# Unpacking 4-bit zeros as bytes, fetching the first tiles' scales tile by tile, and forming weights one tile ahead

## The chip, the cores and the metric

The kernel runs on one core of one Trainium2 chip. A core has TensorE (PE, matrix products, results into the eight banks of PSUM), VectorE (DVE), ScalarE (ACT), GpSimd (POOL) and SyncE (SP), which start work when semaphores reach given counts, and 16 DMA engines fed from queues of SyncE, ScalarE and POOL. The metric is the time of one execution on the device, in microseconds; lower is better.

## The reference

Activations x are 4 x 256 tokens of width 512, in f32. The block is a feed-forward, an attention and the same feed-forward again:

```
x = x + 0.5 * ffn(layernorm(x))
x = x + attention(layernorm(x))     # 32 heads of 16, one shared k and v, causal, ALiBi
x = x + 0.5 * ffn(layernorm(x))

ffn(x): w_gu = dequant(qweight_gu, qzeros_gu, scales_gu, g_idx_gu)     # 512 x 2752: gate 1376, up 1376
        w_d  = dequant(qweight_down, qzeros_down, scales_down, g_idx_down)   # 1376 x 512
        return (silu(x @ gate) * (x @ up)) @ w_d
dequant: W[i,j] = scale[g[i],j] * (wq[i,j] - (zq[g[i],j] + 1))
```

The weights wq and the zeros zq are 4-bit numbers, eight to a 32-bit word. Words of qweight hold eight rows of one column; words of qzeros hold eight columns of one group. Gate/up has 4 groups of scales and zeros, down has 10. Both feed-forwards use the same weights.

## The kernel before

**Precision.** Every f32 product is made of three products of reduced f32 ("f32r"): a high half of each operand and the remainder, its low half. `PARTS` (line 1374) lists them as (weight half, activation half): high-high, low-high, high-low. So each weight tile needs a high half (ScalarE's copy) and a low half (VectorE's subtraction), and so do x and the hidden activations.

**Tiles.** The tokens go in two halves of 512, the 1376 hidden columns in 11 tiles of 128 (the last of 96). `s` 0 and 1 are the halves of the first feed-forward, 2 and 3 those of the second. Gate/up weights live in three buffers, `w_near` (tiles 0 to 2), `w_mid` (3 to 6), `w_far` (7 to 10); the last two are also written to memory and read back for the second feed-forward. All weights are dequantised during s = 0, tile by tile, and stay for the rest.

**Preparation.** ScalarE's queue loads the zeros `zw`, the group numbers and, by DRAM to DRAM, the scales into `s_rows` (`scale_rows`, line 616). VectorE unpacks the zeros into 32-bit `zi` one nibble of each word at a time (`unpack`, line 979, eight instructions a call) and casts the near tiles' to bytes `z8` (line 990); ScalarE casts the rest (lines 743, 745). SyncE writes the bytes to `z_rows` and `d_rows`. POOL then gathers, by indirect DMA, one row of scales and one of zeros for each of the 128 partitions and each of 4 k-tiles (`gather_scales`, `gather_zeros`, lines 520 to 528): eight gathers a section, the near one first; `gather_down` (line 530) is one gather a tile, for scales and zeros of the down weight together. A section's tiles can only be formed when all eight of its gathers have landed (`gathered[n]`).

**Forming a tile.** `gu_weight(j)` (line 899) on VectorE shifts and masks the raw words to nibbles (line 906), subtracts zeros and one into PSUM banks 6 and 7 (line 914), multiplies by the scales (line 917). ScalarE's `gu_high(j)` (line 645) casts to the high half; `gu_low(j)` (line 919) takes the low half and frees the banks. `d_weight`, `d_high`, `d_low` do the same for the down weight in SBUF. `load_raw` and `load_raw_d` on SyncE's queue bring the raw words; both, and in iteration 4 the four loads of x's other half (line 398), stand in one order, and each waits for a buffer.

**The order of s = 0**, written out by hand on each engine. VectorE: first the moments and norm of x (`rstds`, `ffn_xn`), x's low halves (`xt_low`), the unpacking of the other zeros, tiles 0 and 1, then in iteration j tile j+2, the product `h_mul(j)` of silu(gate) and up, down weight j, the low halves. TensorE: transposes of x, then for each j `gate_up(0, j)` (24 matmuls of 128x512: for each k-tile the three parts) and `down(0, j-1)` (12). Gate of tile j+1 waits for `sil_ok`, up for `h_ok` of tile j, since one bank each serves gate and up. Its key lines:

```
            for j in range(2):
                gu_weight(j)
                gu_low(j)
            for j in range(NJ):
                if j + 1 < NJ:
                    if j + 2 < NJ:
                        gu_weight(j + 2)
                    h_mul(0, j)
                    d_weight(j)
```

In iterations 3 to 6 VectorE also takes the moments of the next half's x, in 7 to 9 its inverse deviations.

## Time and profile before

| | |
|---|---|
| Runs of the kernel | 614.86, 614.31, 631.7 us; median 614.86 |
| Profiled execution | 614.43 us, of which the span from first to last instruction is 612.6 |
| TensorE matmuls | 559.6 us busy, 91% of the span, 2968 of them |
| TensorE weight loads | 405.8 us, 66% |
| VectorE | 335.8 us, 55% |
| ScalarE | 160.7 us, 26% |
| POOL | 88.9 us, 15% |
| Mean granted TensorE clock | 0.983 of full speed |
| Moved by DMA | 51.52 MB, mean 84 GB/s |

Busy times are of one execution on one core; a line number such as L922 is that of the kernel's text. Matmuls are pipelined, so a busy TensorE need not be at its peak. The releaser of a wait is inferred from semaphore events.

### The profile page before, as it was taken

Reading aid. Unit: us, or ns where it says so; the run is one execution under the profiler, and the core shown is the slowest. Engines: PE = TensorE matmul, PEld = TensorE weight load, DVE = VectorE, ACT = ScalarE, POOL = GpSimd, SP = SyncE. Lnnn points to the kernel's source line nnn. Section 1 sums busy time; section 2 is a strip of 40 time slices with the busy share of each in tenths; the row PEclk is TensorE's granted clock in tenths of the full one; section 3 lists DMA queues with packets and bytes.
Section 4 is the critical chain, followed back from the end, with each engine's and each line's share of the span. In section 5 each row is a group of like instructions: output and inputs, shape, how many; then the busy total and the mean of one; then the engine's idle time right before and its main releaser. Section 6 shows DMA issues by size and latency. Waiting matters only on the chain.

```text
span 612.6 us, 7685 instructions
## 1 busy us (share of the span) xinstructions
PE 559.6 (91%) x2968; PEld 405.8 (66%) x2968; DVE 335.8 (55%) x705; ACT 160.7 (26%) x286; POOL 88.9 (15%) x113
## 2 busy tenths in 40 slices
PE   1399999999999999979799899699999999999997
PEld 1278777778788667656455344356678887888885
DVE  5888999866311355677467899855411245111112
ACT  1242332322111011134523444464111112111110
POOL 4678000000310000021211222131000000000000
PEclk9999999999999999989889999799999999999999
DMA  7489511099057291205843000000790000100001
GB/s 206 152 251 277 147 31 39 13 247 431 8 102 132 76 120 18 39 2 102 144 87 52 4 2 1 6 1 1 237 294 1 1 0 18 51 2 0 1 0 68
DMA packets 40267, 51.52 MB, mean 84 GB/s; under 512 B 10700, under 2 KB 28214, under 8 KB 39832
## 3 DMA queue, kind: packets, MB, share of 16 engines
q1 hardware_dynamic: 35392, 40.13, 26.5%
q0 software_dynamic: 2656, 10.57, 5.4%
q10 hardware_dynamic: 2184, 0.35, 0.4%
q8 instruction: 23, 0.38, 0.3%
q14 instruction: 12, 0.10, 0.0%
HBM read 35.82 MB, written 15.02 MB: 83 GB/s over the span
## 4 chain that ended last, share of the span: by engine, by line
PE 58%; DVE 9%; ACT 1%; DMA 1%; issue 1%; ACTq 0%; DVEq 0%
PE bank L1395 25%; PE bank L1421 12%; PE bank L1561 4%; PE bank L1487 3%; PE bank L1454 3%; DVE nm L1129 3%; PE bank L1479 3%; PE bank L1533 2%; PE bank L1519 2%; PE bank L1554 2%; DMA qp_b<-two 1%; PE bank L1435 1%; PE bank L1439 1%; DVE stats L843 1%; PE bank L1361 1%
## 5 line engine op out<-in xcount | busy, mean ns | idle before, releaser
L1421 PE MATMUL bank<-w_d,hs 128*128 128x512 f32 (+1 forms) x528 | 131.1, 396 | 3.3 <-DVE w_d L944 1.8
L1421 PEld LDWEIGHTS bank<-w_d,hs 128*128 128x128 f32 (+1 forms) x528 | 97.6, 188 | 27.9 <-issue 5.4
L953 DVE TENSOR_TENSOR hf<-sil,bank 128x512 f32<-128x512 f32 (+1 forms) x44 | 30.1, 684 | 151.9 <-PE bank L1395 151.7
L1395 PE MATMUL bank<-xt,w_far 128*128 128x512 f32 (+1 forms) x384 | 92.5, 394 | 0.0
L1395 PE MATMUL bank<-xt,w_mid 128*128 128x512 f32 x384 | 90.6, 391 | 0.0
L1395 PE MATMUL bank<-xt,w_near 128*128 128x512 f32 x288 | 73.3, 406 | 10.0 <-DVE w_near L922 9.4
L1395 PEld LDWEIGHTS bank<-xt,w_mid 128*128 128x128 f32 x384 | 72.0, 188 | 15.4 <-issue 0.5
L1395 PEld LDWEIGHTS bank<-xt,w_far 128*128 128x128 f32 (+1 forms) x384 | 69.3, 181 | 18.2
L1129 DVE TENSOR_REDUCE nm<-bank 128x2 f32<-128x512 f32 (+1 forms) x96 | 61.7, 685 | 31.5 <-PE bank L1487 31.0
L1395 PEld LDWEIGHTS bank<-xt,w_near 128*128 128x128 f32 x288 | 54.2, 193 | 24.5 <-issue 12.2
L674 ACT CAST hs<-hf 128x512 fp32r<-128x512 f32 (+1 forms) x44 | 27.3, 621 | 130.9 <-DVE hf L953 118.0
L664 ACT ACTIVATE sil<-bank 128x512 f32<-128x512 f32 (+1 forms) x44 | 26.3, 597 | 127.8 <-PE bank L1395 127.4
L959 DVE TENSOR_TENSOR hs<-hf,hs 128x512 fp32r<-128x512 f32 (+1 forms) x44 | 32.5, 739 | 19.4 <-ACT hs L674 19.3
L1361 PE MATMUL bank<-ident,xn 128*128 128x128 f32 x96 | 17.2, 327 | 22.3 <-DVE xn L886 21.8
L1188 DVE RECIPROCAL den<-bank 128x128 f32<-128x128 f32 x32 | 30.4, 949 | 9.6 <-PE bank L1554 9.6
L1454 PE MATMUL bank<-xa,wqkv 128*128 128x256 f32 x128 | 31.5, 397 | 0.0
L1361 PEld LDWEIGHTS bank<-ident,xn 128*128 128x128 f32 x96 | 13.1, 166 | 26.4 <-issue 21.1
L608 POOL TENSOR_SCALAR_AFFINE_SELECT pt_a<-pt_a 128x512 f32<-128x512 f32 x16 | 10.4, 648 | 135.9 <-ACT pt_a L727 135.9
L1479 PE MATMUL bank<-causal,ident_b 128*128 128x256 bf16 (+1 forms) x96 | 22.7, 319 | 7.1 <-DVE nm L1129 6.2
L1454 PEld LDWEIGHTS bank<-xa,wqkv 128*128 128x128 f32 x128 | 24.6, 197 | 6.1 <-issue 2.8
L727 ACT ACTIVATE pt_a<-bank 128x512 f32<-128x512 f32 x32 | 17.4, 596 | 37.2 <-PE bank L1519 37.2
L1561 PE MATMUL bank<-wo,at_t 128*128 128x512 f32 x48 | 25.0, 627 | 0.0
(148 smaller groups left out, 566.5 us busy)
## 6 DMA issues: line engine op xcount, KB each, us to landing
gate_up_part<-w_mid SPq DMA_DIRECT2D x1, 4096.0 KB, 15.5
q_rows<-qst SPq DMA_DIRECT2D x16, 256.0 KB, 4.8
w_mid<-gate_up_part SPq DMA_DIRECT2D x4, 1024.0 KB, 8.3
gate_up_part<-w_far SPq DMA_DIRECT2D x1, 3840.0 KB, 24.0
qp_a<-q_rows SPq DMA_DIRECT2D x24, 128.0 KB, 4.4
w_far<-gate_up_part SPq DMA_DIRECT2D x3, 1024.0 KB, 9.0
raw_d<-in_L_ffn_qweight_down SPq DMA_DIRECT2D x10, 256.0 KB, 3.5
x<-in_L_attn_hidden_states SPq DMA_DIRECT2D x8, 256.0 KB, 5.0
```

The lines of the kernel that those rows point to most:

```text
L664: nc.scalar.activation(sil[0:jw(jt(s, p)), n % 2, :], gate_bank(s, p)[0:jw(jt(s, p)), :], ACT.Silu)\
L674: nc.scalar.copy(hs[0:jw(jt(s, p)), n % 2, 0, :], hf[0:jw(jt(s, p)), n % 2, :]).then_inc(h_hi, 1)
L953: nc.vector.tensor_tensor(hf[0:jw(jt(s, p)), n % 2, :], sil[0:jw(jt(s, p)), n % 2, :], up_bank(s, p)[0:jw(jt(s, p)), :], ALU.mult).then_in ...
L959: nc.vector.tensor_tensor(hs[0:jw(jt(s, p)), n % 2, 1, :], hf[0:jw(jt(s, p)), n % 2, :], hs[0:jw(jt(s, p)), n % 2, 0, :].bitcast(F32), ALU ...
L1129: nc.vector.tensor_reduce(nm[:, min(u, 1), 2 * h0 + s:2 * (h0 + heads) + s - 1:2], bank[6 + s][:, :].rearrange("p (h n) -> p h n", h=heads ...
L1188: st.did(nc.vector.reciprocal(den[:, cols], ps))
L1361: ins = nc.tensor.transpose(ps[:, k * P:(k + 1) * P], xn[:, n % 2, k * P:(k + 1) * P], ident[:, :])
L1395: ins = nc.tensor.matmul(ps[0:jw(j), :], w_gu(a, k, gu, j), xt[:, b, k, :], start=(k == 0 and q == 0), stop=(k == KT - 1 and q == 2))
L1421: ins = nc.tensor.matmul(acc(s, t)[:, :], hs[0:jw(j), n % 2, a, t * P:(t + 1) * P], w_d[0:jw(j), j, b, :], start=(p == 0 and q == 0), stop ...
L1454: ins = nc.tensor.matmul(q_bank(b, h)[:, m * S:(m + 1) * S], wqkv[:, k, (2 * h + m) * P:(2 * h + m + 1) * P], xa[:, k, :], start=(k == 0), ...
L1479: nc.tensor.matmul(ps[:, :, 4 * P // heads - P:], ident_b[:, :], causal[:, :].unsqueeze(1).to_broadcast([P, heads, P]), start=True, stop=F ...
L1561: ins = nc.tensor.matmul(out_bank(b, t)[:, :], normed(b)[:, k, t * P:(t + 1) * P], wo[:, k, :], start=(k == 0), stop=(k == KT - 1))
```

## The change

It has four parts. (1) Zeros are unpacked as bytes: two instructions per matrix shift whole words by 0 and by 4 and mask with 0x0f0f0f0f (`unpack`, with a third column of `shifts` that POOL sets to 4), and two strided byte copies interleave them into `z8`. They stand earlier: all gate/up zeros at the very start, down's after the moments of x; ScalarE's byte copies stand ahead of its casts of the transposed x. (2) The scales and zeros of each near tile get a DRAM tensor of their own, `near_rows[j]`, in which a row holds both; POOL fetches tile 0, 1 and 2 with four gathers each (`gather_near`) into `near_raw`, which lies where `w_far` will be, so that the far gathers wait for the near tiles to be formed (`gu_w` at 3). POOL's order is near 0, near 1, down 0, near 2, down 1 and 2, the middle eight, down 3, the far eight, the other down. (3) Weights are formed one tile ahead instead of two: only tile 0 before the loop, tile j+1 in iteration j; the nibbles are split off as `gu_nibbles`. (4) For s = 0 the products of a gate or up go part by part over the four k-tiles in the order high-high, weight high with x low, weight low with x high (`FIRST`), and the waits for low halves move to the part that needs them.

The diff, cut to its core (declarations of buffers and semaphores left out):

```diff
...
+    near_rows = [nc.dram_tensor(f"near_rows{j}", (G_GU, 2, P + P // 4), F32, kind="Internal").ap()
+                 for j in range(SEC[1])]
...
-            sp.wait_ge(z_bytes[0], 1)
+            sp.wait_ge(z_bytes[0], 2)
             z_near = z8[0:2 * G_GU, 0:SECW[0]].bitcast(F32)
-            sp.dma_start(z_rows[0].rearrange("r (g n) -> (r g) n", g=2), z_near).then_inc(z_ok[0], 16)
-            load_raw(0)
+            for j in range(SEC[1]):
+                sp.dma_start(near_rows[j][:, :, P:].rearrange("r g n -> (r g) n"),
+                             z_near[:, j * P // 4:(j + 1) * P // 4]).then_inc(near_ok[j], 16)
+                if j == 0:
+                    load_raw(0)
+            sp.wait_ge(z_bytes[1], 2)
+            for n in (1, 2):
+                cols = z8[0:2 * G_GU, SEC[n] * P:SEC[n] * P + SECW[n]].bitcast(F32)
+                sp.dma_start(z_rows[n].rearrange("r (g n) -> (r g) n", g=2), cols).then_inc(z_ok[n], 16)
+            sp.wait_ge(z_bytes[2], 2)
+            sp.dma_start(d_rows[:, D:D + D // 4], z8[32:32 + G_D, 0:D].bitcast(F32)).then_inc(d_rows_ok, 16)
             load_raw(1)
             load_raw_d(0)
             load_raw(2)
-            sp.wait_ge(z_bytes[1], 1)
-            for n in (1, 2):
-                cols = z8[0:2 * G_GU, SEC[n] * P:SEC[n] * P + SECW[n]].bitcast(F32)
-                sp.dma_start(z_rows[n].rearrange("r (g n) -> (r g) n", g=2), cols).then_inc(z_ok[n], 16)
-            sp.wait_ge(z_bytes[2], 1)
-            sp.dma_start(d_rows[:, D:D + D // 4], z8[32:32 + G_D, 0:D].bitcast(F32)).then_inc(d_rows_ok, 16)
             load_raw_d(1)
...
+            def gather_near(j):
+
+                pool.wait_ge(near_ok[j], 32)
+                for kt in range(KT):
+                    nc.gpsimd.indirect_dma_start(near_raw[:, j, kt, :, :].rearrange("p g n -> p (g n)"), None,
+                                                 near_rows[j].rearrange("r g n -> r (g n)"), group_of(kt))\
+                        .then_inc(near_in[j], 16)
...
-            pool.wait_ge(s_ok[0], 16)
-            for kt in range(KT):
-                gather_scales(0, kt)
-            pool.wait_ge(z_ok[0], 16)
-            for kt in range(KT):
-                gather_zeros(0, kt)
+            gather_near(0)
             pool.wait_ge(gi_d_in, 32)
             groups(slice(KT, KT + NJ), G_D)
             st.wait()
+            pool.wait_ge(d_rows_ok, 32)
+            gather_near(1)
+            gather_down(0)
+            gather_near(2)
+            gather_down(1)
+            gather_down(2)
             pool.wait_ge(s_ok[1], 16)
+            pool.wait_ge(z_ok[1], 16)
             for kt in range(KT):
                 gather_scales(1, kt)
-                if kt == 0:
-                    pool.wait_ge(z_ok[1], 16)
                 gather_zeros(1, kt)
-                if kt == 1:
-                    pool.wait_ge(d_rows_ok, 32)
-                    gather_down(0)
-            gather_down(1)
-            gather_down(2)
+            gather_down(3)
             pool.wait_ge(s_ok[2], 16)
             pool.wait_ge(z_ok[2], 16)
+            pool.wait_ge(gu_w, SEC[1])
             for kt in range(KT):
                 gather_scales(2, kt)
                 gather_zeros(2, kt)
-            gather_down(3)
             for j in range(4, NJ):
...
+            def near_scales(j):
+
+                act.dma_start(near_rows[j][:, :, 0:P], gu3[:, :, j * P:(j + 1) * P]).then_inc(near_ok[j], 16)
...
-            scale_rows(0, slice(0, SECW[0]), slice(0, SECW[0]))
+            near_scales(0)
...
+            for j in range(1, SEC[1]):
+                near_scales(j)
...
+            act.wait_ge(z_unpacked[0], 2)
+            for e in range(2):
+                nc.scalar.copy(z8[0:2 * G_GU, SECW[0] + e:F:2],
+                               zi[0:2 * G_GU, e, :].bitcast(U8)[:, SECW[0] // 2:F // 2]).then_inc(z_bytes[1], 1)
+            act.wait_ge(z_unpacked[1], 2)
+            for e in range(2):
+                nc.scalar.copy(z8[32:32 + G_D, e:D:2], zi[32:32 + G_D, e, 0:D // 8].bitcast(U8))\
+                    .then_inc(z_bytes[2], 1)
             for t in range(4):
                 xt_high(0, t)
-            act.wait_ge(z_unpacked[1], 8)
-            nc.scalar.copy(z8[0:2 * G_GU, SECW[0]:F], zi[0:2 * G_GU, SECW[0]:F]).then_inc(z_bytes[1], 1)
-            act.wait_ge(z_unpacked[2], 8)
-            nc.scalar.copy(z8[32:32 + G_D, 0:D], zi[32:32 + G_D, 0:D]).then_inc(z_bytes[2], 1)
             gu_high(0)
-            gu_high(1)
             for j in range(NJ):
                 silu(0, j)
-                if j + 2 < NJ:
-                    gu_high(j + 2)
+                if j + 1 < NJ:
+                    gu_high(j + 1)
...
+            def gu_nibbles(j):
+
                 dve.wait_ge(raw_in[j % 3], 32 * (j // 3 + 1))
                 words = raw[:, j % 3, 0:2 * jw(j)]
                 st.did(nc.vector.tensor_scalar(words, words, shifts[:, 0:1], low4[:, :].bitcast(I32),
                                                ALU.logical_shift_right, ALU.bitwise_and))
-                dve.wait_ge(gathered[n], 128)
+
+            def gu_weight(j):
+
+
+
+                n, cols = section(j)
+                words = raw[:, j % 3, 0:2 * jw(j)]
+                dve.wait_ge(*((gathered[n], 128) if n else (near_in[j], 64)))
                 if j >= 1:
                     dve.wait_ge(gu_lo, j)
                 st.wait()
                 q = words.bitcast(U8).rearrange("p (g n k) -> p k g n", g=2, k=KT)
                 w = gu_product(j)
-                st.did(nc.vector.scalar_tensor_tensor(out=w, in0=q, scalar=1.0, in1=zs[n][:, :, :, cols],
+                zeros, scales = zs[n], gu_weights(0, j).bitcast(F32)
+                if n == 0:
+                    scales, zeros = near_raw[:, j, :, :, 0:P], near_raw[:, j, :, :, P:].bitcast(U8)
+                st.did(nc.vector.scalar_tensor_tensor(out=w, in0=q, scalar=1.0, in1=zeros if n == 0 else zeros[:, :, :, cols],
                                                       op0=ALU.subtract, op1=ALU.subtract))
                 st.wait()
-                nc.vector.tensor_tensor(w, w, gu_weights(0, j).bitcast(F32), ALU.mult).then_inc(gu_w, 1)
+                nc.vector.tensor_tensor(w, w, scales, ALU.mult).then_inc(gu_w, 1)
...
-            def unpack(n, rows, lo, hi):
-
-                z = zi[rows, 8 * lo:8 * hi].rearrange("p (w e) -> p w e", e=8)
-                for e in range(8):
-                    nc.vector.tensor_scalar(z[:, :, e], zw[rows, lo:hi], 4 * e, 15,
-                                            ALU.logical_shift_right, ALU.bitwise_and)\
-                        .then_inc(z_unpacked[n], 1)
-
+            def unpack(n, rows, words):
+
+                for e, shift in ((0, shifts[rows, 0:1]), (1, shifts[rows, 2:3])):
+                    nc.vector.tensor_scalar(zi[rows, e, words], zw[rows, words], shift,
+                                            low4[rows, :].bitcast(I32),
+                                            ALU.logical_shift_right, ALU.bitwise_and).then_inc(z_unpacked[n], 1)
+
+            dve.wait_ge(four_ok, 1)
+            st.wait()
             dve.wait_ge(z_in, 16)
-            unpack(0, slice(0, 2 * G_GU), 0, SECW[0] // 8)
-            dve.wait_ge(z_unpacked[0], 8)
-            nc.vector.tensor_copy(z8[0:2 * G_GU, 0:SECW[0]], zi[0:2 * G_GU, 0:SECW[0]]).then_inc(z_bytes[0], 1)
+            unpack(0, slice(0, 2 * G_GU), slice(0, WPR))
+            dve.wait_ge(z_unpacked[0], 2)
+            for e in range(2):
+                nc.vector.tensor_copy(z8[0:2 * G_GU, e:SECW[0]:2],
+                                      zi[0:2 * G_GU, e, :].bitcast(U8)[:, 0:SECW[0] // 2]).then_inc(z_bytes[0], 1)
...
+            dve.wait_ge(zd_in, 16)
+            unpack(1, slice(32, 32 + G_D), slice(0, D // 8))
             rstds(0)
             ffn_xn(0, 0)
             ffn_xn(0, 1)
+            gu_nibbles(0)
+            ffn_xn(0, 2)
+            ffn_xn(0, 3)
+            gu_weight(0)
             for t in range(4):
                 xt_low(0, t)
-                if t < 2:
-                    ffn_xn(0, t + 2)
-            unpack(1, slice(0, 2 * G_GU), SECW[0] // 8, F // 8)
-            dve.wait_ge(zd_in, 16)
-            unpack(2, slice(32, 32 + G_D), 0, D // 8)
-            for j in range(2):
-                gu_weight(j)
-                gu_low(j)
+            gu_low(0)
             for j in range(NJ):
                 if j + 1 < NJ:
-                    if j + 2 < NJ:
-                        gu_weight(j + 2)
+                    gu_nibbles(j + 1)
+                    gu_weight(j + 1)
+                    if j == 0:
+                        gu_low(j + 1)
                     h_mul(0, j)
                     d_weight(j)
-                    if j + 2 < NJ:
-                        gu_low(j + 2)
+                    if j > 0:
+                        gu_low(j + 1)
...
+            FIRST = ((0, 0), (0, 1), (1, 0))
...
-                    pe.wait_ge(xt_lo, 4 * (s + 1))
+                    if s:
+                        pe.wait_ge(xt_lo, 4 * (s + 1))
...
-                for k in steps:
-                    if s == 0 and gu == 0 and k == 0:
-                        pe.wait_ge(gu_hi, j + 1)
-                        pe.wait_ge(gu_lo, j + 1)
+                if s == 0:
+                    for q, (a, b) in enumerate(FIRST):
+                        if gu == 0 and q == 0:
+                            pe.wait_ge(gu_hi, j + 1)
+                        if gu == 0 and q == 1:
+                            pe.wait_ge(xt_lo, 4)
+                        if gu == 0 and q == 2:
+                            pe.wait_ge(gu_lo, j + 1)
+                        for k in range(KT):
+                            ins = nc.tensor.matmul(ps[0:jw(j), :], w_gu(a, k, gu, j), xt[:, b, k, :],
+                                                   start=(k == 0 and q == 0), stop=(k == KT - 1 and q == 2))
+                for k in () if s == 0 else steps:
...
```

## Rows read from the trace of the kernel before

**Rows 1.** Waits of 0 to 45 us: who waited for whom, us, times, longest
```profile
PE bank L1395 <- DVE w_near L922: 9.4, 1, 9.4
```
**Rows 2.** Timeline, all engines, 0 to 40 us: start, us, what, idle before
```profile
5.57 1.30 ACTq L618 DMA_DIRECT2D scale_rows<-in_L_ffn_scales_gu  x2
...
8.46 1.22 POOL L523 DMA_INDIRECT w_near<-scale_rows,gidx  x1 [1.13 <-DMA scale_rows<-in_L_ffn_scales_gu]
...
12.05 1.41 DVE L886 TENSOR_SCALAR xn<-x,mv,rstd 128x512 f32<-128x512 f32 x2
...
19.70 2.18 DVE L983 TENSOR_SCALAR zi<-zw 8x124 int32<-8x124 int32 x16
...
22.84 1.24 DVE L914 SCALAR_TENSOR_TENSOR bank<-raw,zs 128x1024 f32<-128x1024 uint8 x1 [0.51 <-DVE raw L906]
...
25.37 1.01 ACT L648 CAST w_near<-bank 128x1024 fp32r<-128x1024 f32 x1 [2.76 <-DVE bank L917]
```
**Rows 3.** Timeline of TensorE's matmuls, 0 to 140 us
```profile
27.79 12.92 PE L1395 MATMUL bank<-xt,w_near 128*128 128x512 f32 x48 [9.36 <-DVE w_near L922]
...
43.79 5.60 PE L1395 MATMUL bank<-xt,w_near 128*128 128x512 f32 x24
49.23 2.88 PE L1421 MATMUL bank<-w_d,hs 128*128 128x512 f32 x12
51.95 5.60 PE L1395 MATMUL bank<-xt,w_mid 128*128 128x512 f32 x24
...
66.87 3.01 PE L1421 MATMUL bank<-w_d,hs 128*128 128x512 f32 x12 [1.17 <-DVE w_d L944]
...
109.74 2.92 PE L1421 MATMUL bank<-w_d,hs 128*128 128x512 f32 x12
...
118.04 1.03 PE L1361 MATMUL bank<-ident,xn 128*128 128x128 f32 x8
```
**Rows 4.** Timeline of VectorE, 40 to 130 us
```profile
41.27 1.23 DVE L914 SCALAR_TENSOR_TENSOR bank<-raw,zs 128x1024 f32<-128x1024 uint8 x1
...
43.67 0.68 DVE L953 TENSOR_TENSOR hf<-sil,bank 128x512 f32<-128x512 f32 x1
...
46.26 1.22 DVE L922 TENSOR_TENSOR w_mid<-bank,w_mid 128x1024 fp32r<-128x1024 f32 x1
...
51.56 0.68 DVE L953 TENSOR_TENSOR hf<-sil,bank 128x512 f32<-128x512 f32 x1
...
58.75 0.42 DVE L906 TENSOR_SCALAR raw<-raw,shifts,low 128x256 int32<-128x256 int32 x1 [2.16 <-DMA raw<-in_L_ffn_qweight_gu]
...
61.71 0.68 DVE L953 TENSOR_TENSOR hf<-sil,bank 128x512 f32<-128x512 f32 x1
...
104.68 0.68 DVE L953 TENSOR_TENSOR hf<-sil,bank 128x512 f32<-128x512 f32 x1
```
**Rows 5.** Timeline, all engines, 0 to 40 us: POOL's gathers and what meets them
```profile
22.00 0.61 SPq L388 DMA_DIRECT2D zero_rows<-z  x2
...
24.41 0.95 POOL L528 DMA_INDIRECT zs<-zero_rows,gidx  x1 [3.29 <-DMA zero_rows<-z]
...
28.12 1.23 DVE L914 SCALAR_TENSOR_TENSOR bank<-raw,zs 128x1024 f32<-128x1024 uint8 x1
28.17 2.00 POOL L534 DMA_INDIRECT w_d<-down_rows,gidx  x1 [0.30 <-issue]
...
34.37 1.06 POOL L528 DMA_INDIRECT zs<-zero_rows,gidx  x1 [0.30 <-issue]
```
**Rows 6.** By tile, 0 to 45 us: landing of the gathers into zs, then w_near
```profile
DMA to landing us min/median/max: 2.6/3.1/6.2
...
DMA to landing us min/median/max: 4.1/4.4/4.9
```
**Rows 7.** DMA issues of 47.4 to 47.5 us: count, KB each, us to landing
```profile
x<-in_L_attn_hidden_states SPq DMA_DIRECT2D x1, 256.0 KB, 5.1
w_far<-scale_rows,gidx POOLq DMA_INDIRECT x1, 8.2
```

29 lines of the change are left out of this document (18 added, 11 removed).

## The prediction

> **What bounds the kernel now.** I read the page first: TensorE has work in 91% of the span (the table above). It is the bound nearly everywhere, so a change outside its stream pays only where it waits. The waits of the first 45 us name one large stop: 9.4 us before the first gate/up matmul, ended by VectorE's low half of tile 0 [rows 1]. The timeline of that stretch shows what stands ahead of it [rows 2]. POOL gathers the scales and zeros of all three near tiles in eight gathers, the first at 8.46. VectorE unpacks the other zeros from 19.70 (16 instructions, 2.18 us), subtracts the zeros at 22.84 and multiplies; ScalarE casts at 25.37, VectorE takes the low half, and TensorE starts at 27.79 [rows 3]. TensorE's own timeline then shows the stage [rows 3]: a tile is 5.44 us of gate/up (43.79 to 49.23) and 2.72 of down (to 51.95), 8.16 together. The gate/up of the last tile is over at 118.04, where transposes start. VectorE's timeline [rows 4] shows why TensorE still waits 1.17 at 66.87: one tile's VectorE work takes 7.89 (43.67 to 51.56), VectorE stops 2.16 for the raw words of tile 5 at 58.75, and where it also does the next half's moments a tile takes 8.59 (61.71 to 104.68, five tiles). So this stage has two bounds, the start and VectorE, and after 118.04 nothing is touched by the change.
>
> **The start.** The unpacking shrinks: 24 instructions of one nibble each become four shift-and-mask instructions on whole words. The first pair (8x172) now covers all gate/up zeros; a 128x256 one of this form took 0.42 [rows 4] and the 8x124 ones 0.14 apiece [rows 2], so 0.25 to 0.4 each; two byte copies follow. That ends near 4, as before, so nothing is won on the first zeros. Gone is the 2.18 at 19.70; instead two small instructions (0.4) come before the norm, and ScalarE's byte copies (at its 1 ns an element, 1.2 and 0.7 a pair) go ahead of the transposed casts: its DMA issues, two more at 0.65, end at 9, its table load at 10.3, the copies at 12.3, and its first cast was at 14. Tile 0 now needs four gathers, not eight. A gather costs POOL 0.95 plus 0.30 whether it carries scales, zeros or both [rows 5], the first a little more: from 8.46 the fourth is issued at 12.5. It lands after 4.1 to 4.9 (the 3072-byte rows) or 2.6 and more (the 768-byte rows) [rows 6]; with 1280-byte rows I take 3.9, so 16.4. VectorE is by then done: its first two normalised tiles end at 13.5 [rows 2], 0.4 later now, one nibble instruction 0.4, two more tiles 0.7 each, that is 15.8 at least and some 16.1 with their waits for transposes. Subtract and multiply 2.5, to 18.9; cast 1.0 and two handoffs, to 20.1. TensorE needs only the high halves first, so it starts at about 20.2, 7.6 earlier. The four xt low halves (2.5) and the weight's low half (1.2) end at 22.7, inside the first eight matmuls, which are the slow ones: the first 48 took 12.92, and two later sets of 24 take 10.9 [rows 3]. Tile 0 ends near 27.6.
>
> **One tile ahead.** Tile 1 must be formed after tile 0's low half. Its gathers wait on POOL for the down rows in memory: ScalarE's copy ends at 12.3, SyncE issues, and such a write took 2.4 from issue at 22.00 to POOL's release at 24.41 [rows 5], so POOL goes on at about 15.2; 20.2 for the fourth, landed at 23, as VectorE arrives. Tile 1 is complete at 28, tile 0's product, down weight and low halves at 32. Then the new order must hold: a low half ends 3.8 after the product of the tile before (43.67 to 47.48 [rows 4]), and TensorE wants it for its third pass 2.72 + 1.81 = 4.5 after the last tile's end. High halves come 1.1 after a weight, before TensorE's 2.72 of down are over. Both hold while VectorE is less than 0.7 behind. Where VectorE is the bound, TensorE ends a tile 3.7 after the low half: a handoff of 0.1, the gate's third pass 0.91, the up 2.72.
>
> **What is late next: the middle section.** Tile 3 needs eight gathers of four tiles' rows. Before, the last was issued at 34.37 as POOL's 17th and landed unseen before 41.27. Now it is the 23rd: from 15.2 there are 19 (eight near, three down, eight middle). At the bare 1.26 the last starts at 37.9. But some take longer: the one that began at 28.17, 0.05 after a VectorE instruction with two operands in SBUF, took 2.00 and ended 0.82 after that instruction; from 24.41 to 34.37 the pitch was 1.42 with one such in seven [rows 5], which for all 19 would give 40.8. Laying the 19 on VectorE's new order, with that 0.82, I find one or two, so 39.3. Landing: up to 6.2 for zeros [rows 6], but 8.2 where the loads of x run beside it [rows 7], and now these loads (SyncE waits for the down weight of tile 1, about 38) do run beside it. I take 5.2, so 44.5; the ends are 41 (37.9 + 3.1, the zeros' middle value) and 49 (40.8 + 8.2). VectorE would have wanted it at 40.5 to 41.
>
> The Trainium skill (SBUF — State Buffer, "SBUF: two separate sides") says that VectorE and GpSimd share a port pair which an instruction holds alone to its end, among VectorE's those with two SBUF inputs against a GpSimd instruction that reads SBUF. The trace agrees with it, by the 2.00 above. Without such holds the last gather would start at 37.9 and the sum come out 1.4 lower.
>
> **The sum.** Tile 3 subtracted at 44.5 instead of 41.27 [rows 4], but by now VectorE is one product further: product 2 at 46.9 instead of 51.56, 4.7 early. The 2.16 at 58.75 goes: the words of tile 5 are asked for in the same place but wanted one tile (8 us) later. Product 3 is then 6.8 early (54.9). From there both kernels run at VectorE's 8.6; product 8 comes at 98.4 (6.3 early: the narrow last tile's weight, 0.5 cheaper, is no longer ahead of it). Low half of tile 9: +3.8; TensorE ends it 3.7 later, 105.9 against 109.74. With the last tile 8.16 it ends at 114.0 against 118.04: **4.0 us off**, since TensorE, whose tiles ended some 4 us ahead of VectorE's product before, is now 1 us ahead. The 7.6 of the start is not what counts. The rest of the span follows unchanged: norms, transposes, loads of attention weights and spills are all triggered from the end of this stage. The profiled execution took 614.43 (span 612.6), 0.4 under the median of the runs shown; 614.43 − 4.0 = 610.4, with the median's share **610.5**.
>
> **Rivals.**
> (a) The middle gathers land by 41 to 42: then VectorE is never stopped, product 2 comes 3 earlier, and the gain is 6.5 to 7.5: 607.5. For it: the bare issue time. Against: the loads of x at that place, and that it leaves nothing for the two-operand instructions.
> (b) They land at 46 to 48.5: each us is a us; gain 0 to 2.5, 613. For it: the 8.2 landing.
> (c) Slower than before. The queue on POOL stretches: if the ten gathers before tile 3 (two down, eight middle) all took 2.00 + 0.30, as single ones did, they would end 10.4 later, land at 55 and cost 10.5: 621. It decides at 48.5; beyond that each us is a us over 614.4. For it: the upper end of 49 is already past that point. Against: the 1.42 of the stretch most like it, one long gather in seven [rows 5].
> (d) Tile 0 doesn't come earlier: four gathers are as late as eight, because the row of scales and zeros of tile 0 isn't in memory until late. The zeros now leave in pieces of 128 bytes, before 384 bytes; the first gather waited 1.13 for the scales, not for them. Losing all 7.6 puts VectorE at tile 2 at 39.6 and leaves 0.4 of the gain: 614. I see nothing that long; up to 4 us lost by VectorE alone at the start cost nothing, since the middle gathers hide them, while what POOL loses there is lost us for us.
> The Trainium skill (DMA: Bandwidth & Descriptors, "Specifications") says that under 512 bytes the engines read, modify and write. Both kernels' zeros are under it, and no row here separates it from the rest of a landing. Its "Rules for kernel authors" would have small transfers joined into large ones; here the trace shows the price as POOL's 1.26 a gather, four more of them, 5 us on the way to tile 3, and that is in the sum.
>
> **How the numbers follow.** Chances: forecast (landing 42.5 to 46) 0.50; (a) 0.20; (b) 0.15; (c) 0.10; (d) 0.05. The range for 8 in 10 takes (a) whole to 7.4 us off and the forecast and (b), and a little of (c): 607.0 to 615.3. Two per cent (12.3 us) is about what a measurement of this kernel can tell from no change: faster by more would need everything of the start (7.6) and all of TensorE's waits after it (under 2) and more, 0.03; slower by more is the far end of (c), landing after 60, 0.02; within, 0.95.
>
> **What would show it.** In the profile after: the first gate/up matmul at about 20 (19 to 22), its wait under 3.5 us; no wait of VectorE for the words of tile 5; a new wait of VectorE before the subtraction of tile 3, ended by the middle gathers, of about 4 us, at 44.5; eight middle gathers issued up to 39 to 40, those begun in VectorE's two-operand instructions longer; TensorE's second gate/up before the down of tile 0 ends at 33; short waits (0.2 to 0.9) before the third pass in the later tiles; the last gate/up of the stage ending at about 114. Wrong would be: tile 3 without a wait (a), tile 2 late because TensorE or ScalarE stands in VectorE's way, or a loss after 118, where I expect a mere shift.

## The result, and the profile after

Recorded were four executions of each kernel, side by side: the changed kernel 630.62, 632.28, 633.57 and 637.12 us (median 632.92), the kernel before 614.31, 614.86, 631.22 and 631.7. The ratio is 1.031 [1.021, 1.040]: **slower**, where 610.5 was forecast, with 0.02 on slower. Two of four executions of the kernel before had lost some 17 us as well; one of them (631.7) was in the table from the start, and the prediction did not ask what it was. The ratio sets the changed kernel against the two executions near 614 alone; beside the two at 631 it is 1.5 us slower in the median. The experiments below ran the kernel before on six more occasions, each on another chip, and the changed kernel on five of them. On three of these chips no execution shows the loss, and there the ratio is 1.003 [1.001, 1.005], 1.002 [1.000, 1.004] and 1.003 [1.001, 1.006]. So there are two results: a **stop** that comes and goes, and that costs the changed kernel some 7 to 20 us an execution, and without it a change that is worth nothing, or 1 to 2.4 us less than nothing, where 4 us of gain were forecast.

TensorE's timeline of the recorded profile (630.62 us, span 628.8) answers to [rows 3]; its columns are start, duration, engine, line, operation, tiles, count and the idle time before:

```profile
19.62 12.89 PE L1439 MATMUL bank<-xt,w_near 128*128 128x512 f32 x48 [2.46 <-issue]
32.35 2.88 PE L1469 MATMUL bank<-w_d,hs 128*128 128x512 f32 x12
36.05 2.06 PE L1439 MATMUL bank<-xt,w_near 128*128 128x512 f32 x8 [0.82 <-issue]
48.10 4.88 PE L1439 MATMUL bank<-xt,w_near 128*128 128x512 f32 x14 [9.99 <-issue]
...
58.36 0.58 PE L1469 MATMUL bank<-w_d,hs 128*128 128x512 f32 x1 [1.72 <-issue]
...
65.38 3.05 PE L1469 MATMUL bank<-w_d,hs 128*128 128x512 f32 x7 [0.81 <-issue]
68.27 5.72 PE L1439 MATMUL bank<-xt,w_mid 128*128 128x512 f32 x24
```

The start is what was forecast: 19.62 (27.79 before), the down of tile 0 at 32.35. Then, from 38 to 66, there are 10 us of nothing, a short run, and single matmuls a microsecond or two apart. (All 24 matmuls of this tile and all 12 of the down are on record, so it is not a gap in the records.) Nothing that the profile shows releases them ("issue"). ScalarE's timeline:

```profile
34.41 0.60 ACT L688 ACTIVATE sil<-bank 128x512 f32<-128x512 f32 x1 [3.79 <-remote]
...
65.55 0.60 ACT L688 ACTIVATE sil<-bank 128x512 f32<-128x512 f32 x1 [17.98 <-remote]
```

and VectorE's:

```profile
44.31 0.69 DVE L987 TENSOR_TENSOR hf<-sil,bank 128x512 f32<-128x512 f32 x1 [9.59 <-remote]
```

ScalarE waits 3.8 and 18.0 us for gate tiles, VectorE 9.6 for tile 1's up, whose last matmul TensorE has on record before 32.4. "Remote" is the profile's word for a signal without a record of who sent it. The windows of the same profile (length; then busy time and count of PE, its weight loads, DVE, ACT and POOL; granted clock, DMA share, GB/s) show who goes on:

```profile
38.00:44.00 6.00, 0.12 (x1) 0.00 (x0) 0.00 (x0) 0.00 (x0) 4.48 (x6) 0.74 0.85 280
44.00:50.00 6.00, 1.90 (x5) 1.51 (x6) 5.42 (x9) 1.24 (x2) 4.48 (x6) 0.50 0.78 240
...
56.00:62.00 6.00, 2.34 (x4) 0.76 (x3) 0.00 (x0) 0.00 (x0) 4.67 (x5) 0.66 0.98 344
```

POOL issues its gathers at the usual pace, the last of them at 60.96, and the DMA engines move 240 to 344 GB/s, while the three compute engines stand or go in short runs. From 68.3 on the profile is that of the changed kernel on a chip without the stop (a_again, below), 14 to 15 us late.

**Where each execution is.** The start of silu is an event that every trace has, 11 a stage. In us, from ScalarE's timelines:

| start of silu of | before | b_again | a_again | a_third | a_fourth | after, recorded | t_tiles | g_late |
|---|---|---|---|---|---|---|---|---|
| tile 0 | 32.98 | 33.10 | 24.51 | 26.36 | 24.53 | 24.36 | 24.22 | 25.07 |
| tile 3 | 54.87 | 55.30 | 56.77 | 52.20 | 55.97 | 71.30 | 48.75 | 56.33 |
| tile 4 | 64.95 | 68.06 | 65.36 | 60.36 | 64.13 | 79.47 | 56.91 | 64.52 |
| tile 8 | 99.46 | 102.56 | 99.49 | 94.60 | 98.28 | 113.64 | 91.23 | 99.18 |
| tile 10 | 115.46 | 118.52 | 116.73 | 111.91 | 115.61 | 130.89 | 108.68 | 116.44 |
| half 1, tile 0 | 129.80 | 132.87 | 131.91 | 128.62 | 130.73 | 146.09 | 125.46 | 131.61 |
| second feed-forward, tile 0 | 420.48 | 424.42 | 422.41 | 420.44 | 421.91 | 436.64 | 417.15 | 422.78 |
| span | 612.6 | 616.5 | 614.5 | 612.5 | 616.1 | 628.8 | 609.2 | 614.9 |

(b_ is the kernel before, a_ the changed one, once more.) The forecast was −4.0 at tile 10 and from there on. a_third has −3.55 there and loses it by the second feed-forward, a_fourth has +0.15, a_again +1.27. Each column is one execution, and two of one kernel can be 3 us apart, as before and b_again are; a_third's is the fastest of its 12. That the change wins nothing rests on all 36 executions of the three chips, not on a column.

### The profile page after: what moved, and what is told of

Its sections match the earlier page's. It is cut to its first block, busy times and chain, and to the rows that moved or that the text cites. A ratio compares the mean times of both kernels' runs of the same rounds, so it can differ in the third digit from the quotient of the medians.

```text
span 628.8 us, 7679 instructions
## 1 busy us (share of the span) xinstructions
PE 564.7 (90%) x2968; PEld 407.6 (65%) x2968; DVE 333.5 (53%) x686; ACT 161.4 (26%) x288; POOL 90.9 (14%) x118
## 4 chain that ended last, share of the span: by engine, by line
PE 57%; DVE 8%; ACT 1%; DMA 1%; issue 1%; ACTq 0%; DVEq 0%
PE bank L1443 25%; PE bank L1469 11%; PE bank L1609 4%; PE bank L1535 3%; PE bank L1502 3%; DVE nm L1167 3%; PE bank L1527 2%; PE bank L1581 2%; PE bank L1567 2%; PE bank L1602 2%; DMA qp_b<-two 1%; PE bank L1483 1%; PE bank L1487 1%; DVE stats L870 1%; PE bank L1399 1%
## 5 line engine op out<-in xcount | busy, mean ns | idle before, releaser
L1469 PE MATMUL bank<-w_d,hs 128*128 128x512 f32 (+1 forms) x528 | 133.8, 400 | 6.9 <-issue 5.5
L1469 PEld LDWEIGHTS bank<-w_d,hs 128*128 128x128 f32 (+1 forms) x528 | 99.3, 190 | 32.6 <-issue 9.7
L1443 PE MATMUL bank<-xt,w_far 128*128 128x512 f32 (+1 forms) x288 | 69.7, 395 | 0.0
L1443 PE MATMUL bank<-xt,w_mid 128*128 128x512 f32 x288 | 68.2, 392 | 0.0
L1443 PEld LDWEIGHTS bank<-xt,w_mid 128*128 128x128 f32 x288 | 54.0, 188 | 11.7 <-issue 0.5
L1443 PEld LDWEIGHTS bank<-xt,w_far 128*128 128x128 f32 (+1 forms) x288 | 51.9, 181 | 13.6
L1443 PE MATMUL bank<-xt,w_near 128*128 128x512 f32 x216 | 54.7, 401 | 0.7 <-issue 0.7
L993 DVE TENSOR_TENSOR hs<-hf,hs 128x512 fp32r<-128x512 f32 (+1 forms) x44 | 32.5, 738 | 19.4 <-ACT hs L698 19.3
L1439 PE MATMUL bank<-xt,w_near 128*128 128x512 f32 x72 | 20.6, 444 | 16.1 <-issue 16.1
```

The lines of the kernel that those rows point to most:

```text
L993: nc.vector.tensor_tensor(hs[0:jw(jt(s, p)), n % 2, 1, :], hf[0:jw(jt(s, p)), n % 2, :], hs[0:jw(jt(s, p)), n % 2, 0, :].bitcast(F32), ALU ...
L1439: ins = nc.tensor.matmul(ps[0:jw(j), :], w_gu(a, k, gu, j), xt[:, b, k, :], start=(k == 0 and q == 0), stop=(k == KT - 1 and q == 2))
L1443: ins = nc.tensor.matmul(ps[0:jw(j), :], w_gu(a, k, gu, j), xt[:, b, k, :], start=(k == 0 and q == 0), stop=(k == KT - 1 and q == 2))
L1469: ins = nc.tensor.matmul(acc(s, t)[:, :], hs[0:jw(j), n % 2, a, t * P:(t + 1) * P], w_d[0:jw(j), j, b, :], start=(p == 0 and q == 0), stop ...
```

## The experiments

"Before" beside each is the kernel before in the same job on the same chip.

### First job (chip 9): both kernels again, and two halves of the change

> The kernel before, unchanged. Two of its four times so far were 614 and two 631; the kernel after showed 631 to 637 and a stop of the engines between 34 and 66 us. Theory A (a stop that some executions of any version have, and that the change does not cause): this control shows both 614 and some 631 again, and its trace at 631 shows idle TensorE of some 17 us within the first 70 us. Theory B (the change itself makes the stop, the two 631 of before are something else, of the chip): at most one in five above 620 here, all of after's above 628.

> The kernel after, unchanged. Theory A: a part of the executions at 609 to 612, the forecast of the schedule without the stop (forecast 114 us for the end of the stage instead of the 133.5 measured), the others at 630 to 637. Theory B: all at 628 or more.

**b_again** 614.8 (12 runs) against 615.17, ratio 0.999 [0.996, 1.001]. **a_again** 617.18 (614.4 to 619.0, 12 runs), ratio 1.003 [1.001, 1.005]. No stop in either: Theory B, that every execution of the changed kernel has it, falls. That the change has no part in it does not follow; see the fourth job. What a_again shows instead is the step that the forecast put in doubt. VectorE's timeline, to be read against [rows 4]:

```profile
39.98 0.42 DVE L930 TENSOR_SCALAR raw<-raw,shifts,low 128x256 int32<-128x256 int32 x1
47.58 1.23 DVE L948 SCALAR_TENSOR_TENSOR bank<-raw,zs 128x1024 f32<-128x1024 uint8 x1 [7.19 <-DMA zs<-zero_rows,gidx]
```

TensorE's, and one window:

```profile
51.28 8.61 PE L1439 MATMUL bank<-xt,w_mid 128*128 128x512 f32 x24 [5.71 <-ACT w_mid L670]
59.73 2.88 PE L1469 MATMUL bank<-w_d,hs 128*128 128x512 f32 x12
62.45 5.60 PE L1439 MATMUL bank<-xt,w_mid 128*128 128x512 f32 x24
```
```profile
50.00:56.00 6.00, 4.72 (x11) 3.83 (x12) 5.70 (x10) 2.15 (x3) 4.78 (x5) 0.55 0.85 274
```

VectorE waits 7.2 us for the middle rows, which land at 47.58 (44.5 forecast). TensorE, idle 5.7 before it, comes back at the lower of its two clock levels (1.2 GHz; 0.55 of full speed granted in the mean of this window), and 24 matmuls take 8.61 where the next 24 take 5.60: **3.0 us more that no step of the prediction had**. The Trainium skill (TensorE: Matmul & The Clock Gate, "Part 1: The HAM clock gate (the "warmup" mystery)") says that an idle TensorE is gated down to 1.2 GHz; the trace agrees, 8.61 against 5.60.

**p1_bytes**: the kernel before with the unpacking of part 1 alone (both `unpack` calls and ScalarE's copies early, gathers and orders as before).

> Part 1 alone on the kernel before: zeros unpacked as bytes and early, written to memory early; gathers by section, two tiles ahead and the order of products as before. The schedule says the eight near gathers end as before (last issued at 17.7) and the unpacking (2.2 us) leaves VectorE ahead of tile 0; tile 0 is then bound by its gathers, so 1 us or less comes off: 613 to 614.5 without a stop. Theory A: both 613.5 and 631 appear. Theory B with part 1 as the cause: all at 628 or more; with another part as the cause: none.

616.34 (12 runs), ratio 1.001 [0.998, 1.004]. TensorE starts at 27.66 as before (27.79): VectorE waits 2.1 for the rows of the eight near gathers, until 22.71, so these hold it, not the unpacking.

**r4_parts**: the changed kernel with part 4 undone (the first line removed stands for the whole loop; the wait for x's low halves goes back too).

```diff
-                    for q, (a, b) in enumerate(FIRST): ...   # a pass over all k-tiles for each part
+                for k in steps:
+                    if s == 0 and gu == 0 and k == 0:
+                        pe.wait_ge(gu_hi, j + 1)
+                        pe.wait_ge(gu_lo, j + 1)
```

> The kernel after with part 4 undone: products of the first half in the order of before, with the waits for all low halves ahead of the first product. The schedule: TensorE starts at about 22 instead of 19.6, and each tile then waits some 1.8 us more for its low half, 11 tiles, less where TensorE is ahead: +5 to +15 against after. Theory A: two groups again, the lower at 615 to 625. Theory B with part 4 as the cause (its groups of the same waits stop TensorE): the stop is gone and the time is under 626 always.

624.05 (6 runs), ratio 1.016 [1.013, 1.018]. TensorE's timeline:

```profile
23.00 7.52 PE L1434 MATMUL bank<-xt,w_near 128*128 128x512 f32 x24 [6.04 <-DVE w_near L956]
...
81.61 5.72 PE L1434 MATMUL bank<-xt,w_mid 128*128 128x512 f32 x24 [1.24 <-DVE w_mid L956]
```

From tile 2 on every tile waits 1.2 to 2.6 for its low half. With weights one tile ahead, part 4 is worth 6.9 us (624.05 − 617.18): part 3 needs part 4. Neither run tells which part brings the stop, since this chip has none.

### Second job (chip 14): the middle rows

> The changed kernel as it is, on another day's chip if one is given. Theory A (the stop of some 15 us lies in the execution, not in the order of the kernel): 615 to 619 again, or, if this chip has the stop, both it and the kernel before near 631. Theory B (only the changed kernel stops): it is 628 or more while the kernel before stays at 615.

**a_third** 615.99 (614.3 to 618.7, 12 runs) against 614.87, ratio 1.002 [1.000, 1.004]. Its profile is the forecast come true, up to tile 10. VectorE, and TensorE:

```profile
44.67 1.23 DVE L948 SCALAR_TENSOR_TENSOR bank<-raw,zs 128x1024 f32<-128x1024 uint8 x1 [2.86 <-DMA zs<-zero_rows,gidx]
```
```profile
20.86 13.74 PE L1439 MATMUL bank<-xt,w_near 128*128 128x512 f32 x48 [4.14 <-ACT w_near L670]
...
48.36 2.08 PE L1439 MATMUL bank<-xt,w_mid 128*128 128x512 f32 x8 [1.40 <-ACT w_mid L670]
50.97 3.92 PE L1439 MATMUL bank<-xt,w_mid 128*128 128x512 f32 x16 [0.53 <-DVE w_mid L956]
...
108.95 5.70 PE L1439 MATMUL bank<-xt,w_far 128*96 128x512 f32 x24
114.49 1.03 PE L1399 MATMUL bank<-ident,xn 128*128 128x128 f32 x8
```

Rows at 44.67, the last gate/up over at 114.49 (114.0 forecast, 118.04 before). Yet its span is 612.5, that of the recorded profile before 612.6.

**x5_after**, and later **x5_before**: the loads of x one tile later.

```diff
-                if j == 4:
+                if j == 5:
                     for t in range(4, TT):
                         sp.dma_start(x[:, t, :], x_tiles[t]).then_inc(x_in_s[4], 16)
```

> The changed kernel with the four loads of x (1 MB) issued one tile later by SyncE (behind the raw words of tile 5, about 50 us instead of 38). Theory Q (the middle gathers land late because the 16 DMA engines are full from 32 to 50 us, and the x loads take their share of them): the wait for the middle rows ends 2.5 to 3.5 us earlier, near 44.5, the stage's last gate/up ends 2 to 3 earlier, 614 to 615 instead of 617.2. Theory P (the landing only follows POOL's issue, 7 us behind the last one): 47.6 and 617 as before.

615.25 (12 runs), ratio 1.000 [0.998, 1.003]; the rows land at 48.01, no earlier. POOL's last middle gather, in a_again and then in x5_after:

```profile
40.58 0.95 POOL L540 DMA_INDIRECT zs<-zero_rows,gidx  x1 [0.30 <-issue]
```
```profile
40.62 1.43 POOL L540 DMA_INDIRECT zs<-zero_rows,gidx  x1 [0.30 <-issue]
```

The same issue, 7.0 us to VectorE's release with the loads of x beside it and 7.4 without them (a_third, on this chip with them, has 5.75): Theory Q falls for the x loads. P, a fixed 7 us behind the last issue, does not hold either, since in a_third the last one is issued at 38.92 and 5.75 later VectorE goes on. The Trainium skill (DMA: Bandwidth & Descriptors, "Queues, rings and completion order") says that each DMA engine serves the queues it has work for in turn, packet by packet. By that rule 1 MB beside the rows should make them later; x5_after does not show it, and the measurement decides.

**t_tiles** and **t_tiles_x5**: scales and zeros of all eleven tiles fetched like the near ones, four gathers of one 1280-byte row a tile, into a ring of eight places; no section gathers, the down gather of tile j−1 behind tile j (shortened).

```diff
-            for kt in range(KT):
-                gather_scales(1, kt)
-                gather_zeros(1, kt)
+            for j in range(2, NJ):
+                gather_tile(j)          # waits for tile_rows[j], from tile 8 for its place in the ring
+                gather_down(j - 1)
```

> The changed kernel with the scales and zeros of all eleven tiles fetched tile by tile (four gathers of 1280-byte rows each, into a ring of eight places), and no section gathers. Theory Q: tile 3 then waits for 0.65 MB instead of 2.6 MB, VectorE does not wait for it, TensorE has no stop near 46 and no drop of its clock there; the last gate/up of the stage ends at 110 to 113, 607 to 610 in all. Theory V (VectorE's own 8.6 us a tile and POOL's longer gathers take it back): short waits at every tile, 613 to 616. Theory P: tile 3's rows are issued at about 33 instead of 40.6, so it gains as well.

> The same tile by tile kernel with the loads of x one tile later too. Theory Q with traffic no longer full at 40 us: within 0.7 us of the tile by tile kernel. If the DMA engines are still the bound there: another 1 to 2 us faster.

**t_tiles 609.52** (608.5 to 611.0, 6 runs), ratio 0.991 [0.987, 0.994]; with x later 609.03, 0.991 [0.987, 0.994], the same. TensorE's timeline of t_tiles:

```profile
45.83 5.60 PE L1414 MATMUL bank<-xt,w_mid 128*128 128x512 f32 x24
51.27 2.88 PE L1444 MATMUL bank<-w_d,hs 128*128 128x512 f32 x12
53.99 5.60 PE L1414 MATMUL bank<-xt,w_mid 128*128 128x512 f32 x24
...
105.72 5.70 PE L1414 MATMUL bank<-xt,w_far 128*96 128x512 f32 x24
111.26 1.03 PE L1374 MATMUL bank<-ident,xn 128*128 128x128 f32 x8
```

VectorE takes tile 3 at 40.95 without a wait, from tile 3 to the end of the last gate/up no wait of TensorE is over 0.5 us, and its clock stays at the upper level (1.00 granted in every window from 26 to 68 us). So the missing gain lay in the wait for the middle section. The version also moves other gathers (tile 1's no longer waits for the down rows, down's stand further back), and their share is not separated.

### Third job (chip 4): more traffic, and part 3 alone undone

> The changed kernel as it is, once more. If the stop of some 15 us belongs to the kernel it must come in some of these executions too (628 or more); by the 24 executions so far (614 to 619) it does not: 615 to 618, with a wait for the middle rows that ends between 44.5 and 48 and a ratio of 1.001 to 1.004.

**a_fourth** 616.81 (613.6 to 618.8, 12 runs) against 614.39, ratio 1.003 [1.001, 1.006]; rows at 47.58, tile 3's matmuls 7.39.

**d_double**: four more copies of 256 KB, x to a spare place in DRAM, behind the loads of x.

> The changed kernel with 1 MB more of copying (x to a spare place in DRAM) issued right behind the loads of x, at about 40 us. Theory Q (DMA packets of other queues take the middle rows' turns): the rows land 1 to 3 us later, near 48 to 50, and the raw words of tiles 4 and 5 later too, in all 1 to 4 us more than the changed kernel, 617 to 621. Theory S (a full set of DMA engines is what makes the stop of 15 us): 628 or more in some or all executions. Theory P (only POOL's issue counts): no difference.

617.12 (6 runs), ratio 1.005 [1.003, 1.007]: 0.3 us over a_fourth, rows at 47.91. No stop, though the DMA engines moved 331 GB/s in the mean of 30 to 50 us. Theory S falls as it was worded, and Q's 1 to 4 us are not there either. But chip 4 shows no stop in any kernel, so the load is not cleared by this run; the sixth job does that.

**u_two**: the changed kernel with weights two tiles ahead.

```diff
+            gu_nibbles(1)
+            gu_weight(1)
+            gu_low(1)
             for j in range(NJ):
-                    gu_nibbles(j + 1)
-                    gu_weight(j + 1)
+                        gu_nibbles(j + 2)
+                        gu_weight(j + 2)
```

> The changed kernel with weights two tiles ahead again (part 3 undone), high halves first kept. TensorE starts at 20 to 21 as in the changed kernel, but the product of tile 0's down waits behind tile 2's weight, and tile 1's behind tile 3's, whose rows land at 44.5 to 48: TensorE stops longer before 50. My theory: one tile ahead is worth 1 to 4 us there, so 617 to 620. Rival: two tiles ahead gives the slack back at the end of the stage (the last two tiles took 8.98 and 8.33 instead of 8.41 and 7.59), and it is even or 1 us faster than the changed kernel.

618.81 (6 runs), ratio 1.007 [1.004, 1.010], 2.0 over a_fourth. VectorE's waits:

```profile
43.66 1.23 DVE L949 SCALAR_TENSOR_TENSOR bank<-raw,zs 128x1024 f32<-128x1024 uint8 x1 [6.85 <-DMA zs<-zero_rows,gidx]
...
62.31 0.41 DVE L931 TENSOR_SCALAR raw<-raw,shifts,low 128x256 int32<-128x256 int32 x1 [3.33 <-DMA raw<-in_L_ffn_qweight_gu]
```

It wants the middle rows sooner (and has them sooner, 4.2 us behind POOL's last issue at 39.51), and the wait for raw words of [rows 4] is back. But from tile 8's silu to tile 10's it takes 16.0 us as before (102.95 to 118.94), the changed kernel 17.2 to 17.3. The time came out as expected, and the rival's mechanism is there too, though smaller: one tile ahead wins in the middle and gives 1.3 back at the end.

> The kernel before with the four loads of x issued one tile later. VectorE's wait for the raw words of tile 5 (2.2 us at 58.75 in one profile, about 4 in the other) comes behind these loads in SyncE's queue: Theory Q says it shrinks to under 1 us and the kernel gains 1 to 3 us, 612 to 614. Rival: the raw words are issued behind the wait for tile 3's down weight in any case, so it stays as it is, 615.

616.19 (12 runs), ratio 1.004 [1.001, 1.006]: 0.4% slower, and both theories missed. The wait for raw words is gone, but VectorE now waits 3.85 for x itself at 68.61.

### Fourth job (chip 2): the stop

> The changed kernel as it is, on one more chip if one is given. Open is the stop of some 15 us of its first executions. If it comes with a chip or a session, some chip must show it in both kernels (630 to 637 against 631); if it comes with neither here, 614 to 619 and a ratio of 1.00 to 1.005, as on the three chips so far.

> The tile by tile kernel once more, beside the changed kernel on the same chip: if its gain is that of the missing wait for the middle rows and not of a lucky execution, 608 to 611 again, with no wait of VectorE over 1.3 us between 30 and 110 us. If the stop comes on this chip, it tells whether a kernel with less DMA traffic at 40 us has it as well.

> The kernel before with part 4 alone: high halves' products first, in the FFN of half 0. TensorE starts after ScalarE's cast (about 26.5) and not after VectorE's low half (27.7). My theory: VectorE's work a tile stays the bound and the start is given back, 0 to 1.3 us faster, 613 to 615. Rival: the order also hides the low halves of each tile, so it gains 2 us or more.

This chip has the stop, in every kernel. Before: 12 of 18 runs at 613.2 to 617.3, six at 622.7 to 627.8. **a_fifth**: 6 of 6 at 623.1 to 635.6. **q4_before** (the kernel before with `FIRST` in half 0): five of 12 at 612.0 to 615.8, seven at 620.0 to 626.0. The mean of the five is 614.3, that of the twelve before 614.6, so part 4 alone gives nothing (on record is 1.001 [0.997, 1.005], which counts the run at 620.0 in). In its profile, of the run at 622.8, TensorE does start at 26.50, but silu of tile 0 is at 32.92 as before. No trace of the kernel before itself with the stop was kept; q4_before's, with waits for "remote" of 5.8, 6.2 and 8.2 us, is the nearest. **t_again**, the tile by tile kernel: 607.1, 616.7, 620.0, 632.0, 641.3 and 652.0. It has the best execution of all and the worst. In t_again's profile (641.3) VectorE, and the end of POOL's row of gathers:

```profile
70.59 0.69 DVE L962 TENSOR_TENSOR hf<-sil,bank 128x512 f32<-128x512 f32 x1 [25.18 <-remote]
```
```profile
72.92 1.12 POOL L546 DMA_INDIRECT ring_a<-tile_rows,gidx  x1 [0.30 <-issue]
74.36 1.43 POOL L553 DMA_INDIRECT w_d<-down_rows,gidx  x1 [0.30 <-issue]
```

Less DMA traffic did not help (191 and 210 GB/s in the windows from 32 to 44 us, 152 to 164 from 50 to 74, in the midst of the stop). What changed was its length. In the traces with the stop (a_sixth's is from the sixth job), in us:

| | after, recorded | a_fifth | a_sixth | q4_before | t_again |
|---|---|---|---|---|---|
| POOL's row of gathers ends | 61.9 | 62.5 | 63.3 | 59.9 | 75.8 |
| the last wait for "remote" ends | 65.6 | 65.4 | 66.5 | 61.4 | 79.9 |

The last such wait ends 1.5 to 4.1 us behind the row, in all five; earlier ones end while POOL still gathers.

### Fifth and sixth job (chips 7 and 8): POOL silent

**g_plain**: the rows of tiles 3 to 10 and of down 3 to 10 come by plain loads on SyncE's queue, as many bytes to the same places. They leave out the choice of the row: every partition gets the first one and not that of its group, so the weights are wrong and only the time counts. POOL gathers for tiles 0 to 2 only. **g_late** issues the same loads later: the middle section behind the raw words of down 2, the far one behind x. The change, shortened:

```diff
-            for kt in range(KT):                      # POOL
-                gather_scales(1, kt)
-                gather_zeros(1, kt)
+            def plain(dst, rows, p, w):               # SyncE
+                src = bass.AP(rows.tensor, 0, [[0, p], [1, w]])
+                return sp.dma_start(dst, src)
```

> The changed kernel in which the scales and zeros of tiles 3 to 10 and the rows of down 3 to 10 come by plain loads from SyncE, of the same bytes, from a fixed row and not from the rows of the groups; POOL gathers for tiles 0 to 2 only and is done near 30 us. Theory G (the stop of 15 to 25 us goes with POOL's gathers: in the five profiles that have it, it ends when the last of POOL's row of gathers is issued): no stop on any chip, none of its executions over 615. Theory L (the stop comes from the load of the DMA engines, whoever issues it): on a chip where the kernel before has executions of 622 and more, this one has them too. Without a stop it should be 607 to 610, since the middle rows are there before 40 us and VectorE does not wait for them.

(Of the traces kept, four had the stop by then; a_sixth's, below, is the fifth.)

g_plain: 6 of 6 at 622.8 to 626.1, the kernel before 613.9 to 630.0 (9 of 11 over 619, so the chip has the stop). My "none over 615" missed, through my own order of queues: VectorE waits 8.5 for near rows at 30.8 and 8.7 for x at 72.7, both with a DMA as their releaser. There is no wait for "remote" in its one profile. The times alone would not have told this from a stop.

> The plain-load kernel of g_plain (fixed rows instead of the rows of the groups, POOL silent from 30 us) with its loads spread: the middle section behind the raw words of down tile 2 (about 31 us), then the loads of x, then down 4 and 5, the far section and the rest. g_plain's waits of 8.5 us at 31 and 8.7 at 73 were for DMA queued ahead of near rows and of x; they should go, with at most 2 us of wait for the middle rows at 40. Theory G (the stop needs POOL's gathers): on a chip with the stop its executions stay together within 5 us, and at 606 to 613, while the changed kernel beside it is at 623 to 636. Theory L (load of the DMA engines alone): executions of 620 and more there.

> The changed kernel beside g_late on the same chip. On a chip with the stop: 623 to 636 in nearly all executions, the kernel before in a third or more of its own. On one without: 614 to 619, the kernel before 611 to 619.

| chip 8 | runs | us |
|---|---|---|
| kernel before | 17 | 613.5 to 618.3 (9), 620.7 to 627.8 (8) |
| a_sixth | 6 | 630.7 to 636.2 |
| g_late | 12 | 615.7 to 620.2 |

g_late was to be at 606 to 613 and is at 618.0, since it has the changed kernel's wait once more, though SyncE issues the eight loads of the middle rows from 31.2 to 38.9: so this wait does not need POOL's gathers (VectorE and TensorE, then a window):

```profile
47.43 1.23 DVE L963 SCALAR_TENSOR_TENSOR bank<-raw,zs 128x1024 f32<-128x1024 uint8 x1 [6.98 <-DMA zs<-zero_rows]
```
```profile
51.12 7.92 PE L1454 MATMUL bank<-xt,w_mid 128*128 128x512 f32 x24 [5.50 <-ACT w_mid L685]
```
```profile
62.00:68.00 6.00, 6.00 (x28) 4.95 (x28) 5.80 (x9) 1.13 (x3) 0.00 (x0) 1.00 0.99 351
```

The window is the point: 351 GB/s and a DMA share of 0.99, on a chip with the stop, and TensorE works through it. a_sixth beside it, VectorE and POOL:

```profile
66.46 0.69 DVE L987 TENSOR_TENSOR hf<-sil,bank 128x512 f32<-128x512 f32 x1 [16.55 <-remote]
```
```profile
62.39 0.93 POOL L554 DMA_INDIRECT w_d<-down_rows,gidx  x1 [0.31 <-issue]
```

In 12 runs of g_late none is over 5 us above its best; all 6 of a_sixth are at 630.7 and more, where the chips without a stop have medians of 616 to 617, and 8 of 17 of the kernel before are at 620.7 and more. g_late's profile has no wait for "remote". Theory L falls, and of Theory G its main part holds, on this one chip: with POOL's row of gathers gone the stop is gone. What of them it takes is open: POOL at work, its queue, or transfers that go by an index (g_late reads one fixed row).

## Why the prediction was wrong, step by step

**The range and the sign.** Of the rivals none was this: what fails is "the sum", which took waits only for rows, words and engines that the trace named, and so put at nothing what here costs some 16 us (632.92 recorded, medians of 616 to 617 on the chips without the stop). (c), the slower side, wanted POOL's queue stretched to 2.3 a gather and rows at 55; in the recorded profile the pace is 1.26 to 1.6 and TensorE has stopped before the rows are wanted. So the 0.02 on slower came true by another way than its own. The one sign ahead was the 631.7 of the kernel before, a run out of line by 17 us, which vanished in the "median of the runs shown" instead of being a case with a price. What exactly holds the signals back is not shown. The change has a part in it: where there is a stop, all 16 executions of the changed kernel have it and 25 of 50 of the kernel before (2 of 4, 6 of 18, 9 of 11 and 8 of 17). Which part of the change, no run tells; with part 4 alone it was 7 of 12, beside 6 of 18. That it is because TensorE now works beside eight more microseconds of gathers is argued, not shown.

**The start**: right. 19.4 to 21.5 (20.2 forecast), with a wait of 2.4 to 4.2 (under 3.5 forecast; the long ones are where tile 0's rows landed late).

**One tile ahead**: right. The waits before the third pass are 0.2 to 0.5 (0.2 to 0.9 forecast).

**The middle section late**: right in kind, small in size, and this is what the 4 us went on without the stop. Rows at 44.67 in one of three undisturbed profiles, at 47.58 in two: POOL's last issue 40.1 to 40.6 where I took 39.3, and 7.0 us or more to land where I took 5.2. This is rival (b), 46 to 48.5, with 0.15. Its price was wrong too. I had "each us is a us", and the rows land 2.9 later than in a_third; tile 4's silu comes 3.8 (a_fourth) and 5.0 (a_again) later, since behind the longer idle time TensorE runs at the lower clock, 7.39 and 8.61 for 5.60.

**No wait for the words of tile 5**: right; none in a_again, a_third or a_fourth. In u_two it is back.

**The end of the stage**: −4.0 forecast, −3.55 in a_third, and where the rows are in time the steps to it are the forecast's own: VectorE's product 3 at 54.99 (54.9), product 8 at 98.53 (98.4), the last gate/up over at 114.49 (114.0). From tile 8's silu to tile 10's it takes 17.2 to 17.3 for 16.0; u_two, with part 3 undone, takes 16.0, so this is the price of part 3, and the sum had no term of its own for it.

**"The rest of the span follows unchanged"**: wrong. From tile 10's silu to the next half's it takes 14.34 before, 15.18 in a_again, 16.71 in a_third (u_two: 14.36). VectorE's last product comes 0.8 later behind TensorE's last gate/up (4.6 to 4.7 for 3.8), and in a_third TensorE falls to the lower clock in between (0.59 granted from 123 to 126), 4.58 for the last 12 down matmuls (2.98 before). Up to the second feed-forward a_third loses another 1.1, but b_again loses 0.9 there as well, so this need not be the change's. Sum for a_third: −3.55 + 2.4 + 1.1 = 0.0 at the second feed-forward, as in the table. For a_again: +1.27 + 0.84 − 0.2 = +1.9.

**Rivals.** (a) is what t_tiles made true: no stop for the rows, 609.5 (607.5 forecast for it). (d) did not come.

## What to carry to other kernels

A run out of line in the times before is a case of the prediction, with its size and a chance, and not something for a median to hide; and a result of four runs on one chip is one draw of it. When a change brings an engine forward, look for the next transfer that all of a section waits for: fetched tile by tile it costs what one tile needs, fetched by section it costs the whole (2.6 MB in place of 0.65, 7 us of wait in place of none). A wait long enough to drop TensorE's clock costs more than its own length: in four profiles waits of 4.4 to 6.2 us were followed by 24 matmuls that took 7.39 to 8.61 for 5.60, 1.8 to 3.0 more. The tile by tile version is the best of all here, 0.991 [0.987, 0.994], but on the chip with the stop its executions go from 607 to 652; there its row of gathers, and with it the stop, was the longest.

## What was not expected of the hardware

- On four of seven occasions (the recorded one and chips 2, 7 and 8; on 7 by the times alone) signals between the compute engines came late while POOL issued a row of indirect gathers, the longest wait of a trace 8 us (q4_before) to 25 us (t_again), and the last one ended 1.5 to 4.1 us behind the row. The gathers mostly kept their pace of 1.26 us meanwhile. On chips 4, 9 and 14 it came in none of 36 executions of the changed kernel and 89 of the kernel before (b_again's 12 with them).
- Plain loads of as many bytes from SyncE's queue did not do it, at 351 GB/s (g_late, one chip, 12 executions).
- What the landing of eight row gathers depends on stays open. From POOL's last issue to VectorE's release it took 4.2 us (u_two), 5.75 (a_third), 7.0, 7.5 (a_again, a_fourth), 7.4 without the loads of x (x5_after) and 7.7 with 1 MB more (d_double). Leaving 1 MB out or adding it gave values within 0.7 of a_again's and a_fourth's; against a_third, on its own chip, x5_after is even 1.6 longer. In g_late, where plain loads bring the rows, they landed at 47.4 as well, 9.3 us behind SyncE's last issue. The one short landing is the one in which SyncE issued nothing from 36.0 to 48.8; that this is its cause is not shown.
